# Constant matmuls ahead of the waits of TensorE in the first mixture attention

## The chip, the cores and the metric

The kernel runs on one core of one Trainium2 chip. The metric is the time of one execution in microseconds, median of several runs; less is better. TensorE computes the matmuls and transposes, ScalarE (ACT), VectorE (DVE) and GpSimd (POOL) work on the rows between them, and SyncE (SP) issues the transfers.

## What is computed

Eight sequences of 256 tokens with 256 features go through four layers: a gated fusion with a memory of 64 rows, a "mixture" block, a gated cross attention with a feed-forward part, and a second mixture block. The change touches the start of the first mixture block. Its first part is

```
x = rms_norm(hidden_states, ln_in_w)
mixed = where(vm, x @ v_qkv, x @ l_qkv)          # two experts, chosen by token
q, k, v = split(mixed)                            # 16 heads of 16
q, k = apply_rotary(q, k)
ctx = sdpa(q, k, v, causal=True)
hidden_states = residual + where(vm, ctx @ v_dense, ctx @ l_dense)
ci = rms_norm(hidden_states, ln_post_cross_w)     # then the cross attention on the memory
...
```

followed by a cross attention with 64 memory rows and a feed-forward part with two experts. All of it is in f32.

## The kernel before

Everything is kept with the features on the 128 partitions, so a sequence (an "element" e, 0 to 7 in the first mixture block, 8 to 15 in the second) is a tile of 128 x 2 x 256. The four layers run one after another in the main, but within a mixture block the stages of several elements are interleaved: norm (`n0_*`), projections (`q`, `k`, `v`), attention (`first_scores`, `turn_max`, `second_scores`, `values`), cross attention (`memory`, `dense`, `crs_*`, `cross_*`) and feed-forward (`up`, `down`).

The order is written out: each stage has a time in a table (`norm_stages`, `project_stages`, `attend_stages`, `cross_stages`, lines 210 to 597), each element a start, and `whole_order` (line 960) sorts all of them into one list. Every engine walks this list and issues the stages that are its own, in that order (`walk`, line 989). Between engines there are only semaphores: a stage waits (`wait_ge`) for counts of the stages whose results it reads or whose buffers it takes over.

On TensorE the order from the first norm of the first mixture block to its first cross attention is: n0_sum(0), n0_spread(0), q(0), k(0), v(0), n0_sum(1), n0_spread(1), first_scores(0,0), q(1), first_scores(0,1), k(1), first_scores(0,2), v(1), first_scores(0,3), n0_sum(2), n0_spread(2), turn_max(0), second_scores(0,0), second_scores(0,1), values(0,0), second_scores(0,2), values(0,1), second_scores(0,3), first_scores(1,0), values(0,2), values(0,3), first_scores(1,1), q(2), memory(0).

The names and lines that matter below:

- `n0_sum` (line 1450, matmuls at line 1442): sums of squares with the constant matrix `mean_w`, after POOL's addition (line 1241). DVE takes the mean (2233), POOL the power -1/2 (1250), `n0_spread` (1463, transposes at 1447) spreads it over partitions, DVE multiplies (2243) and splits by expert (2247, 2249).
- `q` (1467) and `k` (1482) go through `to_experts` (1421; matmuls at 1433 and, for the first expert, 1426), `v` (1491) through matmuls at 1495. In `q` of element 0, line 1470 reads eight values of the tile `early` into registers of TensorE's sequencer (`pe.value_load`), one for each sequence.
- `first_scores` (1507; 1527 and the causal mask at 1532) are made to find a maximum (DVE 2293), which `turn_max` (1536; transposes at 1545) brings to the other axis, and DVE (2300) subtracts inside the queries. `second_scores` (1548; 1560) are then exponentiated (ACT 2051), masked (POOL `select`, 1283), and multiplied with the values (`values`, 1565; 1577).
- `memory` (1584) is the first use of `crs_bank`, a bank of PSUM, in the mixture block. The loads of x use it before. `att_bank` holds sums, spreads, turned maxima and the attention's results.

Of the kernel before, what the change touches and what calls it, by code (L numbers as in the profile page):

```python
# [29 lines left out]
P = 128  # L30
# [139 lines left out]
def load_stages():  # L170

    at = []

    def put(time, stage, *which):
        at.append((time, stage, *which))

    put(-8637.7284, "x_out")
    put(4848.2942, "x_turn")
    return at


def fuse_stages():

    at = []

    def put(time, stage, *which):
        at.append((time, stage, *which))

    put(-9564.6366, "f_add")
    put(-9564.2232, "f_rstd")  # L190
    put(-780.2099, "f_shift")
    put(-779.9075, "f_sums")
    put(-772.2775, "f_gated")
    put(-771.5608, "f_mean")
    put(-771.0806, "f_y")
    put(-416.5783, "f_exp")
    put(-416.2034, "f_turn_out")
    put(-415.8700, "f_context_out")
    put(-413.5954, "f_tanh")
    put(-412.9521, "f_square")  # L200
    put(1545.6724, "f_scores")
    put(1546.6753, "f_turn")
    put(1547.0006, "f_context")
    put(1547.3799, "f_gate")
    put(1554.5187, "f_sum")
    put(1554.9323, "f_spread")
    return at
# [634 lines left out]
def keys_stages():  # L842

    at = []

    def put(time, stage, *which):
        at.append((time, stage, *which))

    put(-804.7289, "a_keys_out", 0)
    put(-804.4289, "a_keys_out", 1)  # L850
    put(1088.9990, "a_keys", 0)
    put(1089.0990, "a_keys", 1)
    return at
# [48 lines left out]
def final_stages():  # L902

    at = []

    def put(time, stage, *which):
        at.append((time, stage, *which))

    put(-9564.6367, "out_sent")
    put(-24.1953, "out")  # L910
    put(1485.6441, "turn_out")
    return at


def once_stages():

    at = []

    def put(time, stage, *which):
        at.append((time, stage, *which))  # L920

    put(-9125.4755, "p_vec_out")
    put(-9009.7270, "f_mem_out", 0)
    put(2269.6313, "p_one_hot")
    put(2270.2195, "p_trig_out")
    put(2272.2799, "p_seen")
    put(2455.0669, "a_zero")
    put(2634.1904, "f_mem_out", 1)
    put(2641.9461, "f_mem_out", 2)
    put(2642.8294, "f_mem_out", 3)  # L930
    put(4467.6526, "p_vec")
    put(4508.4445, "f_mem", 0)
    put(4596.4685, "p_trig")
    put(4597.0345, "f_mem", 1)
    put(4604.8206, "f_mem", 2)
    put(4605.0045, "f_mem", 3)
    return at
# [22 lines left out]
def whole_order():  # L960

    order = [(time, stage, 0, *which) for time, stage, *which in once_stages()]

    def each(starts, stages, first=0):
        for e in range(B):
            order.extend((starts[e] + time, stage, first + e, *which) for time, stage, *which in stages)

    def by_parity(starts, stages_of, layer):
        for e in range(B):
            order.extend((starts[layer][e] + time, stage, layer * B + e, *which) for time, stage, *which in stages_of(layer, e % 2))  # L970

    each(LOAD_STARTS, load_stages())
    each(FUSE_STARTS, fuse_stages())
    for layer in range(2):
        by_parity(NORM_STARTS, norm_stages, layer)
        by_parity(PROJECT_STARTS, project_stages, layer)
        by_parity(ATTEND_STARTS, attend_stages, layer)
        by_parity(CROSS_STARTS, cross_stages, layer)
        by_parity(FEED_STARTS, feed_stages, layer)
        order.extend((LATE_STARTS[layer][e // 2] + time, stage, layer * B + e, *which) for e in range(1, B, 2)  # L980
                     for time, stage, *which in late_stages(layer))
    each(FINAL_STARTS, final_stages(), B)
    each(GATED_STARTS, gated_stages())
    order.extend((KEYS_STARTS[e // 2] + time, stage, e, *which) for e in range(0, B, 2) for time, stage, *which in keys_stages())
    each(GATED_FF_STARTS, gated_ff_stages())
    return [(stage, e, *which) for _time, stage, e, *which in sorted(order)]
# [8 lines left out]
def program(nc, x_d, ctx_d, pos_d, type_d, media_d, fuse_w, mot_w, ca_w, const_d, out_d):  # L995
    ctx = ExitStack()
    with ctx:
        def sb(name, shape, dt=F32):
            return ctx.enter_context(nc.sbuf_tensor(name, shape, dt))
# [12 lines left out]
        mean_w = sb("mean_w", [P, P])  # L1012
# [155 lines left out]


        order = whole_order()  # L1170
        count = {n: [Count(section[n][e], order, n, e) for e in ENGINES] for n in SECTIONS}
        X_PE, X_ACT, X_DVE, _ = count["x"]
        F_PE, F_ACT, F_DVE, F_POOL = count["f"]
# [5 lines left out]
        OUT_PE, OUT_ACT, _, _ = count["out"]  # L1179
# [42 lines left out]
        with nc.Block() as block:  # L1222
# [151 lines left out]
            def _(pe):  # L1374
# [65 lines left out]
                def sum_squares(sq, out):  # L1440
                    for t in range(TT):
                        last = pe.matmul(out[:, t:t + 1], sq[:, 0, t * P:(t + 1) * P], mean_w[:, 0:1], start=True, stop=True)
                    return last
# [4 lines left out]
                    return last  # L1448

                def n0_sum(e):  # L1450
                    pe.wait_ge(*N0_POOL.did(e, "add"))
                    if e > 0:
                        pe.wait_ge(*N0_DVE.did(e - 1, "y"))
                    if e == 0:
                        pe.wait_ge(*F_ACT.did(0, "m3"))
                        pe.wait_ge(*X_ACT.did(B - 1, "x"))
                    elif e == B:
                        pe.wait_ge(*A_DVE.did(B - 1, "scaled"))
                    elif e % B > 2:
                        pe.wait_ge(*ATT_DVE.did(e - 3, "ctx1"))  # L1460
                    sum_squares(n0_sq, att_bank).then_inc(*N0_PE.does(e, "sumsq"))

                def n0_spread(e):
                    pe.wait_ge(*N0_POOL.did(e, "rstd"))
                    spread(n0_rs, att_bank).then_inc(*N0_PE.does(e, "spread"))

                def q(e):
                    if e == 0:
                        pe.wait_ge(*X_DVE.did(0, "early"))
                        has_early.extend(pe.value_load(early[0:1, b:b + 1]) for b in range(B))  # L1470
                    if e % B == 0:
                        pe.wait_ge(mot_in, 16 * MOT_DMAS * (e // B + 1))
                    if e % B > 3:
                        pe.wait_ge(*free_1(e - 4))
                    elif e % B > 0:
                        pe.wait_ge(*QKV_ACT.did(e - 1, "v1"))
                    if e == B or e == B + 1:
                        pe.wait_ge(*B_ACT.did(e - 2, "gelu2"))
                    pe.wait_ge(*N0_DVE.did(e, "yl"))
                    to_experts(e, ff_bank[1], qkv, 0, n0_yl, n0_yv, N0_DVE.did(e, "yv")).then_inc(*QKV_PE.does(e, "q"))  # L1480

# [52 lines left out]
                    last.then_inc(*ATT_PE.does(e, f"s1{w}"))  # L1534

                def turn_max(e):
                    pe.wait_ge(*ATT_DVE.did(e, "max3"))
                    if e % B + 2 < B:
                        pe.wait_ge(*N0_DVE.did(e + 2, "y"))
                    if e > 0:  # L1540
                        pe.wait_ge(*ATT_DVE.did(e - 1, "ctx1"))
                    for t in range(KT):
                        for i in range(TT):
                            at = t * S + i * P
                            last = pe.transpose(att_bank[:, at:at + P], neg_max[:, 2 * t + i, :], ident)
                    last.then_inc(*ATT_PE.does(e, "nm"))

                def second_scores(e, w):

                    t, par = w // 2, w % 2  # L1550
                    pe.wait_ge(*ATT_DVE.did(e, f"qa{par}"))
                    if w == 0:
                        if e > 0:
                            pe.wait_ge(*CRS_DVE.did(e - 1, "cmax1"))
                    else:
                        pe.wait_ge(*ATT_ACT.did(e, f"exp{w - 1}"))
                    for i in range(TT):
                        for j in range(4):
                            r = slice(32 * j, 32 * j + 32)
                            last = pe.matmul(row_banks[:, j, S * i:S + P * i], k_one[e % 2][par][r, t, i * P:(i + 1) * P],  # L1560
                                             q_one[e % 2][par][r, t, i * P:S], start=(i == 0), stop=(i == 1),
                                             skip_group_check=True)
                    last.then_inc(*ATT_PE.does(e, f"s2{w}"))
# [1042 lines left out]
```

## Time and profile before

| | us |
|---|---|
| median of 3 runs | 1384.76 |
| lowest, highest | 1384.41, 1391.71 |
| the profiled execution | 1382.84 |
| its span, first to last instruction | 1380.9 |
| TensorE busy in the span | 1306.9 (95%) |
| VectorE, ScalarE, GpSimd busy | 764.5, 473.6, 452.1 |
| mean granted clock of TensorE | 0.98 |

All times inside the execution are microseconds from its span's start. TensorE's busy time counts a matmul until its modelled end, so consecutive matmuls overlap; the chain of work gives the time that a group of them takes on the path. The granted clock is a share of 2.4 GHz: 1.00 is 2.4 GHz, 0.50 is 1.2 GHz, and a value between the two is a stretch with some of both. "Idle before" is the time that an engine stood still ahead of an instruction, with the engine that released it.

### The profile page before, as it was taken

Reading aid. Unit: us, or ns where it says so; the run is one execution under the profiler, and the core shown is the slowest. Engines: PE = TensorE matmul, PEld = TensorE weight load, DVE = VectorE, ACT = ScalarE, POOL = GpSimd, SP = SyncE. Lnnn points to the kernel's source line nnn. Section 1 sums busy time; section 2 is a strip of 40 time slices with the busy share of each in tenths; the row PEclk is TensorE's granted clock in tenths of the full one; section 3 lists DMA queues with packets and bytes.
Section 4 is the critical chain, followed back from the end, with each engine's and each line's share of the span. In section 5 each row is a group of like instructions: output and inputs, shape, how many; then the busy total and the mean of one; then the engine's idle time right before and its main releaser. Section 6 shows DMA issues by size and latency. Waiting matters only on the chain.

```text
span 1380.9 us, 25903 instructions
## 1 busy us (share of the span) xinstructions
PE 1306.9 (95%) x10931; PEld 1047.3 (76%) x10931; DVE 764.5 (55%) x1361; ACT 473.6 (34%) x785; POOL 452.1 (33%) x559
## 2 busy tenths in 40 slices
PE   7978899999999998999999999998899999999988
PEld 5755677787887776888888888876678777787767
DVE  4455576666666656354354444446667566666543
ACT  3323333423324222244445543433332333323321
POOL 1143444444344342311111111324434344334332
PEclk9978999999999999999999999999999999999999
DMA  9010000000001001110000000011000000000000
GB/s 324 8 61 1 2 2 2 1 2 2 2 2 47 2 5 48 50 60 1 0 1 1 1 0 1 1 42 42 1 2 1 9 9 2 1 17 2 1 16 17
DMA packets 19901, 27.29 MB, mean 20 GB/s; under 512 B 3432, under 2 KB 15552, under 8 KB 19520
## 3 DMA queue, kind: packets, MB, share of 16 engines
q1 hardware_dynamic: 19008, 24.20, 5.2%
q8 instruction: 99, 1.62, 0.5%
q10 hardware_dynamic: 768, 1.26, 0.3%
q14 instruction: 26, 0.21, 0.1%
HBM read 23.35 MB, written 2.10 MB: 18 GB/s over the span
## 4 chain that ended last, share of the span: by engine, by line
PE 84%; DVE 6%; ACT 5%; POOL 3%; issue 2%; ACTq 0%; DVEq 0%; POOLq 0%
PE bank L1433 6%; PE bank L1723 6%; PE bank L1688 5%; PE bank L1693 5%; PE bank L1577 5%; PE bank L1933 4%; PE bank L1940 4%; PE bank L1897 4%; PE row_banks L1527 4%; PE row_banks L1837 3%; PE row_banks L1560 3%; PE bank L1495 3%; PE bank L1712 3%; PE bank L1426 3%; PE row_banks L1532 2%; ACT room L2051 2%
## 5 line engine op out<-in xcount | busy, mean ns | idle before, releaser
L1283 POOL TENSOR_SCALAR_AFFINE_SELECT room<-room 128x1024 f32<-128x1024 f32 x64 | 70.7, 1107 | 185.3 <-ACT room L2051 185.3
L2293 DVE TENSOR_REDUCE room<-row_banks 128x4 f32<-128x512 f32 (+1 forms) x128 | 116.4, 952 | 23.1 <-PE row_banks L1532 22.8
L2051 ACT ACTIVATE room<-row_banks 128x1536 f32<-128x1536 f32 x64 | 92.9, 1451 | 90.0 <-PE row_banks L1560 90.0
L1723 PE MATMUL bank<-room,down_w 128*128 128x256 f32 x384 | 95.9, 391 | 0.5 <-DVE room L2393 0.5
L2307 DVE RECIPROCAL room<-bank 128x256 f32<-128x256 f32 x32 | 56.1, 1754 | 59.3 <-PE bank L1577 59.3
L2083 ACT ACTIVATE room<-bank 128x256 f32<-128x256 f32 x96 | 36.4, 383 | 148.6 <-PE bank L1693 137.6
L1245 POOL TENSOR_TENSOR room<-room 128x256 f32<-128x256 f32 x32 | 24.5, 767 | 173.0 <-ACT room L2063 173.0
L1723 PEld LDWEIGHTS bank<-room,down_w 128*128 128x128 f32 x384 | 70.4, 192 | 14.0 <-issue 4.9
L1357 POOL TENSOR_TENSOR room<-room 128x512 f32<-128x512 f32 x32 | 33.7, 1070 | 133.1 <-DVE room L2495 132.9
L1560 PE MATMUL row_banks<-room 32*128 32x256 f32 (+1 forms) x1024 | 62.1, 357 | 9.7 <-ACT room L2051 4.6
L1560 PEld LDWEIGHTS row_banks<-room 32*128 32x128 f32 x1024 | 48.9, 190 | 27.6 <-issue 15.6
L2376 DVE SCALAR_TENSOR_TENSOR room<-room,bank 128x256 f32<-128x256 f32 x96 | 39.9, 415 | 50.4 <-ACT room L2083 50.4
L1433 PE MATMUL bank<-room,qkv 128*128 128x256 f32 x256 | 64.0, 394 | 2.7 <-DVE room L2249 2.5
L2063 ACT ACTIVATE room<-x_all 128x512 f32<-128x512 f32 x32 | 20.2, 631 | 135.3 <-DVE x_all L2362 96.2
L1527 PE MATMUL row_banks<-room 32*128 32x128 f32 (+1 forms) x1024 | 62.9, 362 | 2.0 <-ACT room L2051 1.7
L1837 PE MATMUL row_banks<-room,wq 128*128 128x256 f32 x256 | 61.0, 382 | 0.0
L1940 PE MATMUL bank<-room,down_w 128*128 128x256 f32 x256 | 60.4, 380 | 0.0
L1933 PE MATMUL bank<-room,up_w 128*128 128x256 f32 x256 | 58.8, 382 | 1.0 <-ACT room L2169 1.0
L1897 PE MATMUL bank<-room,wo 128*128 128x256 f32 x256 | 59.6, 381 | 0.0
L1577 PE MATMUL bank<-room 128*32 128x256 f32 (+1 forms) x1024 | 55.9, 337 | 0.8
L1433 PEld LDWEIGHTS bank<-room,qkv 128*128 128x128 f32 x256 | 48.0, 196 | 10.5 <-issue 3.5
L1933 PEld LDWEIGHTS bank<-room,up_w 128*128 128x128 f32 x256 | 47.4, 190 | 9.3 <-ACT room L2169 2.5
(243 smaller groups left out, 3022.4 us busy)
## 6 DMA issues: line engine op xcount, KB each, us to landing
out_x<-wq SPq DMA_DIRECT2D x8, 256.0 KB, 2.4
qkv<-in_L_xattn_v_qkv SPq DMA_DIRECT2D x2, 768.0 KB, 5.6
qkv<-in_L_xattn_l_qkv SPq DMA_DIRECT2D x2, 768.0 KB, 8.6
gate_w<-in_L_xattn_v_gate SPq DMA_DIRECT2D x2, 640.0 KB, 8.0
gate_w<-in_L_xattn_l_gate SPq DMA_DIRECT2D x2, 640.0 KB, 7.4
up_w<-in_L_xattn_v_up SPq DMA_DIRECT2D x2, 640.0 KB, 6.1
up_w<-in_L_xattn_l_up SPq DMA_DIRECT2D x2, 640.0 KB, 6.4
down_w<-in_L_xattn_v_down SPq DMA_DIRECT2D x2, 640.0 KB, 6.0
```

What stands on the lines that cost most here:

```text
L1283: pool.affine_select(out=diagonal, in_=diagonal, compare_op=ALU.is_ge, fill=0.0, base=0, pattern=[[0, 8], [1, P]], channel_multiplier=-1)\
L1433: pe.matmul(out[:, t * S:(t + 1) * S], w[:, 1, k, at + t * P:at + (t + 1) * P], y_l[:, k, :], start=(t == k == 0), stop=False, skip_group_ ...
L1527: pe.matmul(row_banks[:, j, P * i:P + S * i], q_one[e % 2][par][r, t, i * P:(i + 1) * P], k_one[e % 2][par][r, t, 0:P * (i + 1)], start=(i ...
L1560: last = pe.matmul(row_banks[:, j, S * i:S + P * i], k_one[e % 2][par][r, t, i * P:(i + 1) * P], q_one[e % 2][par][r, t, i * P:S], start=( ...
L1577: last = pe.matmul(att_bank[32 * j:32 * j + 32, at + i * P:at + S], half if of_sums else v_pad[e % 2][:, i, 8 * t + 2 * j + par, :], probs ...
L1723: return pe.matmul(ff_bank[0][:, t * S:(t + 1) * S], down_w[:, f, t * P:(t + 1) * P], hid[:, i, :], start=(i == t == 0), stop=(i == UPS - ...
L1837: last = pe.matmul(row_banks[:, u, j * S:(j + 1) * S], wq[:, k, at:at + P], a_y[:, k, :], start=(k == 0), stop=(k == KT - 1))
L1897: last = pe.matmul(crs_bank[:, t * S:(t + 1) * S], wo[:, k, t * P:(t + 1) * P], a_context[:, k, :], start=(k == t == 0), stop=(k == GT - 1 ...
L1933: last = pe.matmul(ff_bank[(u + 1) % 2][:, j * S:(j + 1) * S], w1[:, k, at:at + P], b_y[:, k, :], start=(k == 0), stop=(k == KT - 1))
L1940: last = pe.matmul(crs_bank[:, t * S:(t + 1) * S], w2[:, k, t * P:(t + 1) * P], b_hid[:, k, :], start=(k == t == 0), stop=(k == GT - 1), s ...
L2051: act.activation(probs[w % 2], row_banks[:, :, 0:3 * P], ACT.Exp).then_inc(*ATT_ACT.does(e, f"exp{w}"))
L2293: last = dve.tensor_reduce(dst, row_banks[:, :, P * i:P + S * i], X, ALU.max, negate=True)
```

## The change

A helper `hold(n, ...)` issues n matmuls whose two operands are both `mean_w`, 128x128, into the first 128 columns of `crs_bank`. Nothing reads the result; `memory(0)` and later stages start new sums there. It issues them only for stages that stand between n0_sum(0) and memory(0) in the order, both excluded. The calls stand ahead of the stage's own waits, except in `q`, where the call stands behind the value loads and all waits but the last one.

```
+        lone = {key: n for n, key in enumerate(order)}
...
                 def n0_sum(e):
+                    hold(4, "n0_sum", e)
                     pe.wait_ge(*N0_POOL.did(e, "add"))
...
+                def hold(n, *key):
+                    if lone["n0_sum", 0] < lone[key] < lone["memory", 0]:
+                        for _ in range(n):
+                            pe.matmul(crs_bank[:, 0:P], mean_w[:], mean_w[:], start=True, stop=True)
+
                 def n0_spread(e):
+                    hold(3, "n0_spread", e)
                     pe.wait_ge(*N0_POOL.did(e, "rstd"))
...
                     if e == B or e == B + 1:
                         pe.wait_ge(*B_ACT.did(e - 2, "gelu2"))
+                    hold(6 if e == 0 else 3, "q", e)
                     pe.wait_ge(*N0_DVE.did(e, "yl"))
...
                 def turn_max(e):
+                    hold(4, "turn_max", e)
                     pe.wait_ge(*ATT_DVE.did(e, "max3"))
...
                 def second_scores(e, w):
+                    hold(4, "second_scores", e, w)
 
                     t, par = w // 2, w % 2
                     pe.wait_ge(*ATT_DVE.did(e, f"qa{par}"))
```

## Rows read from the trace of the kernel before

**Rows 1.** The page: granted clock in 40 slices, and the chain by engine.

```profile
PEclk9978999999999999999999999999999999999999
PE 84%; DVE 6%; ACT 5%; POOL 3%; issue 2%; ACTq 0%; DVEq 0%; POOLq 0%
```

**Rows 2.** Busy time by stretch: columns in the first line.

```profile
core 0: us, PE busy (x) PEld busy (x) DVE busy (x) ACT busy (x) POOL busy (x), PEclk, DMA share, GB/s
84.90:87.30 2.40, 0.00 (x0) 0.00 (x0) 2.23 (x4) 0.00 (x0) 0.00 (x0) 0.50 1.00 413
91.00:91.50 0.50, 0.50 (x6) 0.50 (x4) 0.00 (x0) 0.00 (x0) 0.00 (x0) 0.76 0.00 0
98.00:101.00 3.00, 0.88 (x6) 0.71 (x6) 1.36 (x2) 3.00 (x9) 1.73 (x3) 1.00 0.00 0
101.00:101.50 0.50, 0.18 (x6) 0.05 (x4) 0.31 (x1) 0.38 (x1) 0.00 (x0) 0.98 0.00 0
104.50:105.00 0.50, 0.50 (x3) 0.41 (x2) 0.50 (x2) 0.00 (x0) 0.00 (x0) 0.60 0.14 33
115.10:118.30 3.20, 2.02 (x25) 1.30 (x24) 0.95 (x3) 3.08 (x8) 1.43 (x2) 1.00 0.00 0
118.50:119.00 0.50, 0.38 (x2) 0.04 (x1) 0.50 (x1) 0.50 (x1) 0.00 (x0) 0.55 0.00 0
128.50:129.00 0.50, 0.50 (x16) 0.18 (x8) 0.00 (x0) 0.10 (x1) 0.34 (x1) 0.71 0.00 0
132.20:135.60 3.40, 1.75 (x35) 1.23 (x30) 1.72 (x2) 1.45 (x1) 1.80 (x2) 1.00 0.02 5
163.00:169.50 6.50, 4.86 (x50) 2.99 (x50) 0.88 (x2) 2.90 (x2) 2.18 (x2) 0.50 0.00 0
995.00:1003.00 8.00, 5.95 (x33) 4.01 (x34) 6.52 (x13) 0.74 (x2) 3.80 (x4) 0.57 0.00 0
```

**Rows 3.** The value loads of line 1470, and the instructions in time beside them.

```profile
L1470 PEldq TENSOR_LOAD <-early x8: 301/306/496, 84.1 to 86.9; - x8
84.15 0.69 PE L1447 MATMUL bank<-const,room 128*128 128x128 f32 x2 [1.03 <-POOL room L1250]
86.51 0.69 DVE L2249 TENSOR_TENSOR room<-room 128x512 f32<-128x512 f32 x1
87.38 0.76 PE L1433 MATMUL bank<-room,qkv 128*128 128x256 f32 x1 [2.54 <-DVE room L2249]
```

**Rows 4.** TensorE's instructions in time: start, duration, count, [idle before, releaser].

```profile
99.08 0.61 PE L1442 MATMUL bank<-mean_w,room 128*128 128x1 f32 x4 [1.74 <-POOL room L1241]
101.48 1.67 PE L1527 MATMUL row_banks<-room 32*128 32x128 f32 x16 [0.32 <-ACT room L2041]
...
103.90 2.39 PE L1433 MATMUL bank<-room,qkv 128*128 128x256 f32 x8
...
116.71 0.61 PE L1442 MATMUL bank<-mean_w,room 128*128 128x1 f32 x4 [0.20 <-POOL room L1241]
...
120.17 1.09 PE L1545 MATMUL bank<-const,room 128*128 128x128 f32 x4 [1.29 <-DVE room L2243]
122.10 1.67 PE L1560 MATMUL row_banks<-room 32*128 32x256 f32 x16 [0.84 <-DVE room L2300]
125.42 1.67 PE L1560 MATMUL row_banks<-room 32*128 32x256 f32 x16 [1.66 <-ACT room L2051]
...
129.30 0.94 PE L1560 MATMUL row_banks<-room 32*128 32x256 f32 x16
...
131.90 0.94 PE L1560 MATMUL row_banks<-room 32*128 32x256 f32 x16 [0.22 <-ACT room L2051]
```

**Rows 5.** Chain of work (start, us, what), and one select of POOL.

```profile
266.54 1.98 PE bank L1712 x16
127.09 2.28 PE bank L1577 x32
179.89 1.30 PE bank L1577 x32
125.35 1.10 POOL L1283 TENSOR_SCALAR_AFFINE_SELECT room<-room 128x1024 f32<-128x1024 f32 x1 [7.06 <-ACT room L2051]
```

More of the change, by code:

```diff
@@ L1170, in program @@
         order = whole_order()
+        lone = {key: n for n, key in enumerate(order)}
         count = {n: [Count(section[n][e], order, n, e) for e in ENGINES] for n in SECTIONS}
@@ L1450, in n0_sum @@
                 def n0_sum(e):
+                    hold(4, "n0_sum", e)
                     pe.wait_ge(*N0_POOL.did(e, "add"))
@@ L1461, in n0_sum, with hold @@
                     sum_squares(n0_sq, att_bank).then_inc(*N0_PE.does(e, "sumsq"))
+                def hold(n, *key):
+                    if lone["n0_sum", 0] < lone[key] < lone["memory", 0]:
+                        for _ in range(n):
+                            pe.matmul(crs_bank[:, 0:P], mean_w[:], mean_w[:], start=True, stop=True)
                 def n0_spread(e):
+                    hold(3, "n0_spread", e)
                     pe.wait_ge(*N0_POOL.did(e, "rstd"))
@@ L1478, in q @@
                         pe.wait_ge(*B_ACT.did(e - 2, "gelu2"))
+                    hold(6 if e == 0 else 3, "q", e)
                     pe.wait_ge(*N0_DVE.did(e, "yl"))
@@ L1536, in turn_max @@
                 def turn_max(e):
+                    hold(4, "turn_max", e)
                     pe.wait_ge(*ATT_DVE.did(e, "max3"))
@@ L1548, in second_scores @@
                 def second_scores(e, w):
+                    hold(4, "second_scores", e, w)
                     t, par = w // 2, w % 2
```

## The prediction

> **What bounds the kernel now.** The page comes first. The chain of work that ended last is 84% TensorE, and the granted clock is at full speed in nearly every slice; the only slices below nine tenths lie early, between about 70 and 175 us [rows 1]. So time is lost to the clock only in a few places, and time on TensorE's path is mostly paid one for one. Next I cut the early part into short stretches to see where the clock changes level [rows 2]. It is low already over 84.9 to 87.3, rises inside 91.0 to 91.5, is low again from 101.5 to inside 104.5 to 105.0, falls inside 118.5 to 119.0 and rises inside 128.5 to 129.0, and is low over 163.0 to 169.5. Low is 1.2 GHz (0.50), high 2.4 GHz (1.00). Taking each change inside its row by the row's mean clock, the first low ends at about 91.3, the second is 101.5 to 104.9 and the third 118.6 to 128.8. Ahead of the second one TensorE was busy for 0.88 of 3.0 us, and ahead of the third for 2.02 of 3.2 us [rows 2]. These lows are what the products could remove. Last I read the instructions of TensorE in order with the idle time ahead of each [rows 3, 4], since a product is free only if it lies in such an idle time.
>
> **Which products run where.** The order of stages puts these between the first sum and the first cross attention: spread(0) 3, q(0) 6, sum(1) 4, spread(1) 3, q(1) 3, sum(2) 4, spread(2) 3, turn_max(0) 4, second_scores(0, 0 to 3) 4 each, q(2) 3: 49 in all.
>
> **Price of one.** A product is a 128x128 f32 weight load and a 128-column f32 matmul. The nearest row is the run of sixteen such matmuls of L1712 at the high clock: 1.98 us, 0.124 us each [rows 5]. At the low clock I take twice that, 0.248, since the same second-score group costs 1.67 us low and 0.94 high [rows 4]. So three cost 0.37, four 0.50, six 0.74 at the high clock. All 49 would be 6.1 us high, 12.2 low; nothing hidden is the upper bound, all hidden the lower.
>
> **Products that gaps hide.** Each spread waits 1.03 us for the power on POOL (one of three alike stands in rows 3): three products fit even at the low clock (0.74). Sum(1) waits 1.74 us, four fit. Turn_max(0) waits 1.29, second_scores(0,0) 0.84, second_scores(0,1) 1.66 [rows 4]: 0.50 each fits at the high clock; at the low one (0.99) the middle of these would stick out by 0.15. Cost: nothing. Without that cover each would cost its 0.37 or 0.50.
>
> **Products that nothing hides.** q(0) looks as if it had a gap of 2.54 us, but the sequencer is not free in it: has_early reads eight values, 0.30 us each, the first at 84.1 and the last at 86.9 [rows 3], so they end at about 87.2. The six products stand behind them in the order. The splitting on DVE that q(0) waits for also ends at 87.20 (86.51+0.69) [rows 3]. So the gap is covered by the loads, and the six start when q(0) would have. They run at the low clock, 1.49 us. The first low stretch has begun before the first product, and the 2.4 us without any TensorE work [rows 2] stay, so I let the clock rise at 91.3 as before. Then 1.49 us of low work is pushed out and an equal amount of q(0) moves beyond the rise, at half its price: the delay is 0.74. The bounds are 0 (the rise comes earlier by that much) and 1.49 (it moves along). From v(0) to the first scores of element 0 the chain carries this 0.74. These scores would start at 102.2 in place of 101.48, still in the second low. That stretch then does 0.74 us less of slow work, which refunds 0.37.
> q(1) and q(2) follow the group before them with no idle time (one of the two stands in rows 4): 0.37 each. Sum(2) waits only 0.20 [rows 4]: 0.50 less 0.20 is 0.30, and what waits behind it is spread(2), and on DVE the mean, which stands ahead of the last maximum of element 0 and so of turn_max. Second_scores(0,2) has no idle time ahead of it: 0.50. Its exp on ACT waits with it. Second_scores(0,3) has 0.22 [rows 4]: 0.28. Sum of what is paid: 0.74 - 0.37 + 0.37 + 0.30 + 0.50 + 0.28 + 0.37 = 2.19 us.
>
> **What the clock gives back.** First low: nothing, as said. Second low: I expect it to stay. In the 4 us between v(0) and the first scores (97.3 to 101.5) TensorE gets seven products, 0.87 us, beside 0.88 us of its own small matmuls in 98 to 101 [rows 2], and most of it remains without work. If it did go, the scores would take what such a group takes at the high clock, 0.94 rather than 1.67 [rows 4], and the rest of the stretch, 1.8 us, would halve: in all 1.7 us less, minus the 0.37 already counted. Third low: I expect it to go. Ahead of it TensorE had 2.02 of 3.2 us; the four products of sum(2) and three of spread(2) close 0.87 of the rest, and the following idle times (1.29, 0.84, 1.66) get 0.50 each. Its price, on the path: turn_max 1.09 against some 0.55 (half), 0.55; second_scores(0,0) 1.67 against 0.94, 0.73; second_scores(0,1) ends 0.73 earlier too, but values(0,0) waits for the select on POOL, which is what comes late next (exp ends at about 125.3, select takes 1.10 from 125.35 on [rows 5], so values could start near 126.5 in place of 127.09): 0.58. Values(0,0), 2.28 against 1.30 for the same 32 matmuls at the high clock [rows 5]: 0.98. Together 2.84 us.
> **Net: 2.19 - 2.84 = -0.65 us.** The path behind is PE's again, so it carries to the end.
>
> A rule of the skill speaks about the matmuls that lie in these gaps already. Rows show the clock low over transposes that are busy for part of a gap [rows 4]. The Trainium skill, "TensorE: Matmul & The Clock Gate", Part 4, says that transposes don't count as TensorE activity the way matmuls do. By that the ordinary products here do more for the clock than the transposes beside them, which agrees with the third low going; no row of before separates the two.
>
> **The time.** The profiled execution took 1382.84 us (span 1380.9 and 1.9 around it), 1.9 below the median of the runs shown, 1384.76. By the profile's own time the change gives 1382.2; on the median 1384.1. I forecast the median, 1384.1.
>
> **Rivals.**
> (a) *The products cost, and the clock is no better* (slower). One mechanism, at the third low: it stays, or returns a few us later. For it: each idle time there (1.29, 0.84, 1.66) gets only 0.50 of products, so TensorE still stands still between the groups. Against it: at 132.2 to 135.6 the clock stayed high over idle times of 0.22 and 1.65 between the same groups (1.75 of 3.4 us busy) [rows 2]. Then the 2.19 are paid, and 0.15 for second_scores(0,0): +2.3, 1387.1. It decides as soon as the clock returns less than 2.2 us.
> (b) *More lows go.* The second (1.7 - 0.4 = 1.3 us), and the one at 163.0 to 169.5, in which TensorE is busy for 4.86 us at half speed [rows 2], 2.4 us at most. It lies behind the last product, and only a shift in time can move it: ahead of it DVE holds TensorE up for 3 us, which argues that it stays. Both: -0.65 - 1.3 - 2.4 = -4.4, 1380.4.
> (c) *The lows are not tied to the program.* The profiled execution alone shows where the clock changed; it was 1.9 us faster than the median, and other runs may have their lows elsewhere. The Trainium skill, the same page, "What's actually happening", says the point of change is not set by the kernel's start and varies. A shift of the later part by half a us can then also make or unmake a low such as the one within 995.0 to 1003.0 [rows 2], where TensorE was busy for 5.95 us at a mean clock of 0.57: each is worth 1.7 us or so either way. That puts the time at 1381 to 1389 with no trend.
> (d) *The change does not do what it says at q(0)*: its six products lie behind the value loads and not in the gap. That is in my sum already; if the loads ended earlier, or the low ended earlier because of them, the time would be 0.4 to 0.7 lower, 1383.5.
>
> **How the numbers follow.** Forecast (with d) 0.50, (a) 0.22, (b) 0.18, (c) 0.10. About 0.5% (6.9 us) is what a measurement of this kernel can tell from no change. Neither -4.4 nor +2.3 reaches it; only several lows together with (c) do, in either direction: faster 0.05, slower 0.04, same 0.91. The range goes from (b) to (a) with one further low of 1.7: 1380.4 to 1388.8. Its ends leave 2 in 10 out, mostly for disturbances like the third run of before, 1391.71.
>
> **What would show it.** In the profile of after: matmuls of 128x128 with mean_w in the bank of the cross attention, 49 of them; q(0)'s first true matmul at about 88.6 and not 87.4 (right: the loads cover the gap); the clock rising near 91.3 and low again near 101.5 to 104.9; high from 104.9 past 128.8, with turn_max at 0.55 and second scores at 0.94 (wrong: 1.09 and 1.67); second_scores(0,2) starting 0.5 after values(0,0) ends; q(2) about 0.7 us earlier than 139.95. Wrong in kind would be idle times that grow by what the products take, a low clock at new places behind 170, or a product price far from 0.12.

## The result and the profile after

| | before | after |
|---|---|---|
| median, 12 runs each | 1384.45 us | 1388.64 us |
| lowest, highest | 1383.31, 1392.04 | 1384.81, 1389.82 |
| the profiled execution (its span) | 1382.84 (1380.9) | 1386.58 (1384.6) |
| TensorE matmuls in the trace | 10931 | 11029 |

The ratio is 1.0025, with a 95% interval of 1.0014 to 1.0035: the change costs some 3.5 us, clear of noise and below the 0.5% that I had called telling. The two medians differ by 4.2 us, and the two profiled executions, one of each kernel, by 3.7 us. These two can be compared piece by piece. The twelve times of after fall in two groups, five from 1384.8 to 1386.6 with a mean granted clock of 0.984 to 0.986 and seven from 1388.6 to 1389.8 with 0.982 or 0.983. The profiled one is the slowest of the first group, so its trace doesn't show what the second group adds.

The page of after, its granted clock in 40 slices and the first line of the chain:

```profile
PEclk9989899999999999999999999999999999999999
PE 84%; DVE 6%; ACT 4%; POOL 3%; issue 2%; DMA 0%; SPq 0%; ACTq 0%; DVEq 0%; POOLq 0%
```

They answer [rows 1]: the same bound, and no slice below eight tenths where before had one at seven. The stretches of after answer [rows 2] (columns as there):

```profile
79.30:92.60 13.30, 10.40 (x39) 8.66 (x39) 5.19 (x12) 0.00 (x0) 3.01 (x5) 0.50 0.42 158
93.00:136.90 43.90, 39.30 (x399) 32.38 (x398) 21.84 (x34) 15.98 (x26) 17.64 (x16) 1.00 0.00 1
134.20:137.00 2.80, 1.22 (x20) 0.88 (x20) 0.25 (x1) 1.44 (x1) 1.09 (x1) 1.00 0.00 0
137.00:140.50 3.50, 3.50 (x43) 1.98 (x44) 1.83 (x2) 0.00 (x0) 0.00 (x0) 0.53 0.03 5
167.80:174.60 6.80, 6.33 (x66) 4.20 (x66) 0.88 (x2) 1.78 (x2) 2.19 (x2) 0.51 0.00 0
```

The clock is high without a break from 93.0 to 136.9: both lows that the products surround, near 101 and 118, are gone. The first is as long as before. A new one runs from 137.0 to 140.5, and the one that was at 163 is at 168. So up to the cross attention the clock did better than forecast, one low more gone against a short new one, and the time did worse.

Where it went is in the line of the products and in the chain (start, us, what). First the products' own row, all from the matmul call inside `hold` at L1468 (durations min/median/max in ns, first and last start):

```profile
L1468 PE MATMUL bank<-mean_w x98: 273/275/561, 83.2 to 143.5; 128*128 128x128 f32 x98
```

```profile
85.28 2.19 issue
87.47 2.90 PE bank L1468 x12
90.37 3.01 PE bank L1434 x8
...
105.10 0.67 PE bank L1468 x6
...
118.03 0.89 PE bank L1468 x8
...
122.12 0.63 PE bank L1555 x4
122.75 0.89 PE bank L1468 x8
123.64 0.93 PE row_banks L1571 x16
...
128.78 1.09 PE bank L1468 x8
129.86 0.86 PE row_banks L1571 x16
130.73 1.44 PE bank L1588 x32
132.17 1.09 PE bank L1468 x8
...
137.26 4.41 PE bank L1588 x64
...
143.08 0.67 PE bank L1468 x6
```

The 49 products are 98 matmuls in the trace. The six of q(0) are "x12" and take 2.90 us; four are "x8" and take 0.89, 0.22 each. An f32 matmul is two records here, each with its own weight load (98 weight loads too). A transpose in f32 is one: the two that line 1447 issues are x2 in [rows 3]. I had read "L1712 x16" of [rows 5] as sixteen products at 0.124; by the loops of that line (2 tiles, 2 weight matrices, 2 halves of the contraction) they are eight at 0.248.

How far the execution of after lies behind that of before, at starts of the same work. All but the first row are read from the two chains; the cross attention is taken from the second group of matmuls of memory(0), L1594 in before and L1605 in after. The first row is ahead of the first product; its lines, of before and of after:

```profile
82.10 1.01 PE L1442 MATMUL bank<-mean_w,room 128*128 128x1 f32 x4
82.35 1.01 PE L1443 MATMUL bank<-mean_w,room 128*128 128x1 f32 x4
```

| start of | before | after | behind by |
|---|---|---|---|
| n0_sum(0) | 82.10 | 82.35 | 0.25 |
| q(0) | 87.38 | 90.37 | 2.99 |
| first scores of 0 | 101.48 | 103.62 | 2.14 |
| next first scores | 107.12 | 108.64 | 1.52 |
| turn_max(0) | 120.17 | 122.12 | 1.95 |
| second_scores(0,0) | 122.10 | 123.64 | 1.54 |
| values(0,0) | 127.09 | 127.27 | 0.18 |
| second_scores(0,3) | 131.90 | 133.25 | 1.35 |
| values(0,2) | 135.97 | 137.26 | 1.29 |
| q(2) | 140.11 | 143.75 | 3.64 |
| the cross attention | 142.90 | 146.54 | 3.64 |
| the end | 1380.9 | 1384.6 | 3.7 |

Two things made it: the products that nothing covered, and 1.67 us for the new low (values(0,2) and (0,3): 4.41 for 2.74). What the second and the third low gave back was not enough for both: the lag falls by 0.62 from the first scores of 0 to the next, with the 0.67 of q(1)'s products paid inside, and by 1.77 from turn_max(0) to values(0,0). 0.25 us of the lag has nothing to do with the products, since it is there before the first of them. By the cross attention the loss is complete.

### The profile page after: what moved, and what is told of

The parts are those of the page before. It is cut to its first block, busy times and chain, and to the rows that moved or that the text cites. A ratio compares the mean times of both kernels' runs of the same rounds, so it can differ in the third digit from the quotient of the medians.

```text
span 1384.6 us, 26096 instructions
## 1 busy us (share of the span) xinstructions
PE 1317.5 (95%) x11029; PEld 1058.5 (76%) x11029; DVE 764.6 (55%) x1361; ACT 474.1 (34%) x785; POOL 452.9 (33%) x559
## 4 chain that ended last, share of the span: by engine, by line
PE 84%; DVE 6%; ACT 4%; POOL 3%; issue 2%; DMA 0%; SPq 0%; ACTq 0%; DVEq 0%; POOLq 0%
PE bank L1434 6%; PE bank L1734 6%; PE bank L1699 5%; PE bank L1588 5%; PE bank L1704 5%; PE bank L1944 4%; PE bank L1951 4%; PE bank L1908 4%; PE row_banks L1536 4%; PE row_banks L1848 3%; PE row_banks L1571 3%; PE bank L1504 3%; PE bank L1723 3%; PE bank L1427 3%; PE row_banks L1541 2%; PE row_banks L1882 2%
## 5 line engine op out<-in xcount | busy, mean ns | idle before, releaser
L1588 PE MATMUL bank<-room,const 128*32 128x256 f32 (+1 forms) x1024 | 54.7, 332 | 0.0
```

The lines of the kernel that those rows point to most:

```text
L1588: last = pe.matmul(att_bank[32 * j:32 * j + 32, at + i * P:at + S], half if of_sums else v_pad[e % 2][:, i, 8 * t + 2 * j + par, :], probs ...
```

## The experiments

Each kernel has its own runs of before beside it on the same chip, and only the ratio compares kernels: the medians of before were 1383.66 beside e1 to e4, 1383.72 beside e5 to e8, 1384.61 beside e9 to e11 and 1383.43 beside e12. Two theories were put against each other. P: the loss is the price of the products that no gap covers, at twice what I had taken. C: it is a matter of where the clock falls, and only by chance related to what is paid.

| kernel | median, us | ratio to before | 95% interval | n0_sum(0) | cross attention | from the one to the other | from there to the end |
|---|---|---|---|---|---|---|---|
| before | 1384.45 |  |  | 82.10 | 142.90 | 60.80 | 1238.0 |
| the change | 1388.64 | 1.0025 | 1.0014, 1.0035 | 82.35 | 146.54 | 64.19 | 1238.1 |
| e1 covered products only | 1382.79 | 0.9996 | 0.9987, 1.0005 | 82.50 | 142.82 | 60.32 | 1237.8 |
| e2 uncovered only | 1392.74 | 1.0069 | 1.0055, 1.0083 | 82.37 | 149.04 | 66.67 | 1237.9 |
| e3 q(0)'s six ahead of the loads | 1383.27 | 0.9997 | 0.9983, 1.0010 | 80.91 | 141.52 | 60.61 | 1238.1 |
| e4 16 at k(1) | 1387.24 | 1.0028 | 1.0018, 1.0039 | 82.64 | 147.35 | 64.71 | 1238.0 |
| e5 covered and early six | 1379.72 | 0.9976 | 0.9962, 0.9991 | 81.02 | 137.20 | 56.18 | 1237.9 |
| e6 the same, and first_scores(1,0) | 1377.98 | 0.9963 | 0.9950, 0.9977 | 82.21 | 138.38 | 56.17 | 1237.8 |
| e7 the same, and the fusion | 1377.92 | 0.9965 | 0.9953, 0.9977 | 81.97 | 138.42 | 56.45 | 1241.4 |
| e8 all in bf16 | 1386.47 | 1.0024 | 1.0015, 1.0033 | 81.93 | 144.62 | 62.69 | 1237.9 |
| e9 without q(0)'s six | 1386.52 | 1.0021 | 1.0011, 1.0030 | 81.69 | 145.14 | 63.45 | 1238.6 |
| e10 the early six only | 1385.73 | 1.0012 | 0.9996, 1.0027 | 82.94 | 146.01 | 63.07 | 1242.3 |
| e11 e6 again | 1382.10 | 0.9982 | 0.9967, 0.9998 | 82.02 | 138.26 | 56.24 | 1238.0 |
| e12 the change and first_scores(1,0) | 1389.24 | 1.0038 | 1.0026, 1.0050 | 82.51 | 144.46 | 61.95 | 1242.5 |

The last four columns are from each kernel's one profiled execution, which is any one of its runs. n0_sum(0) stands ahead of the first product (in e7 only, some stand ahead of it), and its start still lies between 80.91 and 82.94 from one execution to another, though the kernels do the same up to there. So what a kernel does to the stretch with the products is read from the last column but one, not from where the cross attention starts. Behind the cross attention eleven of the fourteen executions take the same 1237.8 to 1238.6 us, and those of e7, e10 and e12 take 1241.4 to 1242.5.

**The price.** All products of the change out, sixteen ahead of k(1), between two groups at the high clock:

```
                 def k(e):
+                    if e == 1:
+                        hold(16, "k", e)
```

> None of the change's products; 16 of them stand ahead of k(1), between two full groups of matmuls at the high clock. This measures the price by itself. By the corrected count (two passes per f32 product, 0.22 us): 3.6 us above before. By the prediction's 0.124: 2.0 us above before.

The chain of e4 around them:

```profile
108.87 0.54 PE row_banks L1540 x4
109.41 3.57 PE bank L1467 x32
112.98 1.73 PE bank L1434 x8
```

3.57 us for sixteen, 0.223 each, and the time went up by 0.28%, 3.9 us (interval 0.18 to 0.39%, 2.5 to 5.4 us). From n0_sum(0) to the cross attention the profiled execution took 3.91 us longer than that of before. The price is twice 0.112, and it is paid in full: nothing behind gives it back.

**Covered and uncovered apart.** e1 keeps the 25 products of which a gap covers all or nearly all:

```
-                    hold(4, "n0_sum", e)
+                    hold(4 if e == 1 else 0, "n0_sum", e)
...
-                    hold(6 if e == 0 else 3, "q", e)
...
-                    hold(4, "second_scores", e, w)
+                    hold(4 if w < 2 else 0, "second_scores", e, w)
```

> Only the 25 products of the changed kernel that a gap covers stay (spread(0), sum(1), spread(1), spread(2), turn_max(0), second_scores(0,0) and (0,1)); the 24 that stand where TensorE has other work are left out. Theory P (the loss is the price of the uncovered products, about 0.22 us each at the high clock and 0.48 at the low): at most 0.3 us is paid, and if the lows near 101 and 118 us still go, the time is 1 to 4 us below the kernel before, ratio 0.997 to 0.999. Theory C (the loss is where the clock falls afterwards, whatever is paid): within 1 us of before or above it.

e2 is the other half: the calls of e1 out, and in their place only `hold(4 if e == 2 else 0, "n0_sum", e)`, the call in `q`, and `hold(4 if w > 1 else 0, "second_scores", e, w)`.

> Only the 24 products that no gap covers (q(0) 6, q(1) 3, sum(2) 4, second_scores(0,2) and (0,3) 4 each, q(2) 3). Theory P: all of the price and little of the clock, so slower than the full change: 5 to 7 us above before, ratio 1.004 to 1.005. Theory C: the same lows as before or others by chance, 0 to 4 us above before, not above the full change.

Three stretches of e1, then two of e2:

```profile
102.60:105.60 3.00, 3.00 (x22) 1.80 (x17) 2.44 (x5) 0.00 (x0) 0.00 (x0) 0.50 0.00 0
107.00:132.00 25.00, 22.37 (x265) 17.54 (x263) 13.44 (x20) 10.20 (x15) 9.70 (x9) 1.00 0.01 1
133.20:136.40 3.20, 3.20 (x35) 1.55 (x32) 1.14 (x2) 0.00 (x0) 0.64 (x1) 0.50 0.02 5
```

```profile
102.20:108.80 6.60, 6.23 (x33) 4.61 (x34) 4.08 (x6) 0.82 (x2) 0.11 (x1) 0.50 0.01 2
126.00:132.70 6.70, 5.06 (x64) 3.30 (x56) 1.48 (x3) 2.90 (x2) 1.95 (x2) 0.50 0.00 0
```

In e1 the second low stays and the third is gone, exchanged for a shorter one at 133 where before had none. It is as fast as before within noise. P had said 1 to 4 us less, and C within 1 us of before: C's number came true. From the first sum to the cross attention it took 0.48 us less than before: the new low takes most of what the old one gave. In e2 both lows stay, and it is 0.7% slower, 9 us, more than P's 5 to 7 and far from C's 0 to 4. Its profiled execution, 1388.88, is the fastest of its five runs. There the stretch with the products took 5.87 us longer, which is P's number; the other four runs (1392.4 to 1393.2) took some 4 us more, and no trace shows where. So the uncovered half is the loss; 5.9 of e2's 9 us are seen to be the products'.

**The six of q(0).** e3 moves them ahead of the value loads, e9 leaves them out, e10 keeps them early and nothing else.

```
                 def q(e):
                     if e == 0:
+                        hold(6, "q", e)
+                    if e == 0:
                         pe.wait_ge(*X_DVE.did(0, "early"))
                         has_early.extend(...)
...
-                    hold(6 if e == 0 else 3, "q", e)
+                    if e:
+                        hold(3, "q", e)
```

> The full change with the six products of q(0) ahead of the eight value loads. Theory P: they then run in the 2.5 us in which the sequencer reads values, 2.9 us of low-clock work of which some 2.5 is covered; q(0) starts near 88 and not 90.4, and the time is 1.5 to 2.5 us below the full change. Theory C: no change beyond 1 us unless the first low ends earlier.

> The full change without the six products of q(0), 43 left. If those six cost only their own time, 2.9 us of low-clock work of which part is given back after the rise, this lies 1.5 to 2.5 us below the full change, near 1386.5 (ratio 1.001 to 1.002). If the place ahead of the value loads helped e3_early6 also by ending the first low sooner, e3_early6 stays 2 to 3 us below this one. If both are equal, the gain of e3_early6 was the removal alone.

> The kernel before with only the six products ahead of the value loads. If they end the first low sooner by themselves, q(0) takes 1 to 1.7 us less and the time is 1 to 2 us below before, ratio 0.9985 to 0.9995. If they need the three of spread(0) beside them, the low lasts as before and the 0.4 us that stick out are lost, ratio 1.000.

e3's value loads, its products and q(0) in time, the clock around them, and e3's own new low:

```profile
L1480 PEldq TENSOR_LOAD <-early x8: 296/302/492, 83.1 to 85.8; - x8
```

```profile
83.20 0.64 PE L1448 MATMUL bank<-const,room 128*128 128x128 f32 x2
83.63 2.77 PE L1468 MATMUL bank<-mean_w 128*128 128x128 f32 x12
86.35 2.10 PE L1434 MATMUL bank<-room,qkv 128*128 128x256 f32 x8
```

```profile
83.80:86.30 2.50, 2.50 (x13) 2.30 (x11) 2.26 (x4) 0.00 (x0) 0.00 (x0) 0.50 1.03 421
86.50:87.00 0.50, 0.50 (x3) 0.45 (x4) 0.00 (x0) 0.00 (x0) 0.00 (x0) 0.86 1.04 442
131.00:134.30 3.30, 3.30 (x32) 1.66 (x36) 0.87 (x2) 0.00 (x0) 0.88 (x1) 0.50 0.02 5
```

Once the products stand ahead of them, TensorE works through the twelve matmuls while its sequencer reads the eight values: the loads start at 83.1, the products run from 83.63, and q(0) follows without a gap. In before q(0) starts 5.28 us behind the start of n0_sum(0), in the change 8.02 and in e3 5.49. In before it runs at the low clock for 3.75 us (chain), in e3 it takes 2.06, since the clock rises near 86.6; all five traces with these six and the three of spread(0) have 2.06 to 2.34. That is worth more than the removal, as the runs show: e9, with the six left out, gains 0.04% on the change, e3 0.28%, 3.9 us. For e9 1.5 to 2.5 us had been expected, for e3 the same; from n0_sum(0) to the cross attention they took 0.74 and 3.58 us less than the change. The six are not enough by themselves: in e10's profiled execution the first low lasts to 89.5 or a little more, the second is longer than in before, and one comes at 137.5 to 141.0 with no product near it. Its time is that of before or a little over it. That execution, 1390.26, is one of the slower ones of e10, whose median is 1385.73, so these lows are not those of most of its runs:

```profile
80.00:89.50 9.50, 7.96 (x30) 6.42 (x30) 5.19 (x12) 0.00 (x0) 2.90 (x5) 0.50 0.47 179
100.00:107.00 7.00, 6.47 (x30) 4.31 (x31) 4.08 (x6) 1.12 (x2) 0.41 (x1) 0.51 0.01 2
120.50:130.50 10.00, 6.85 (x68) 4.64 (x68) 3.20 (x6) 2.90 (x2) 1.96 (x2) 0.50 0.00 0
```

**Shorter products.** e8 takes `ident_bf` for both operands of all 49.

> The full change with all 49 products in bf16 (the identity of bf16 on both sides): one pass each rather than two, so about 0.06 us at the high clock. Theory P: the uncovered ones cost a quarter to a half of what they did, so 2 to 5 us below the full change, 1384 to 1386; if the clock falls as in the full change, the lows near 101 and 118 us stay away. Theory C: the time depends on the lows alone and stays near 1388; with shorter products the lows may come back.

```profile
L1468 PE MATMUL bank<-ident_bf x49: 216/219/314, 82.8 to 141.6; 128*128 128x128 bf16 x49
101.20:104.40 3.20, 2.99 (x24) 2.12 (x25) 2.52 (x5) 0.11 (x1) 0.00 (x0) 0.50 0.00 0
121.60:128.30 6.70, 5.57 (x60) 3.93 (x64) 1.90 (x3) 2.90 (x2) 1.22 (x2) 0.50 0.00 0
135.30:138.50 3.20, 3.20 (x35) 1.72 (x36) 1.83 (x2) 0.00 (x0) 0.12 (x1) 0.50 0.02 5
```

One record a product, and a quarter to a half of the price (the four of sum(2): 0.22 us in its chain). But the low at 101 is back and most of that at 118, a new one follows at 135, and the ratio is that of the full change within noise. P had the price right and the clock wrong; what the products cost less, the clock takes back for the most part. In the profiled executions 1.5 us are left of it from n0_sum(0) to the cross attention (62.69 us for 64.19).

**Which products remove which low.** The second low, near 101, is gone in the seven traces with six f32 products at q(0), in either place, and the seven of sum(1) and spread(1) (the change, e3, e5, e6, e7, e11, e12). It is there in e1 and e9, which have the seven alone, in e2 and e10, which have the six alone, and in e8, whose products are short. So it takes both; why the six help over 10 us later is not shown. A new low of some 3 us between 131 and 141 comes in the change, e1, e3, e8, e9 and e10.

**Only what is covered.** e5 is e1 with the six of e3. e6 adds `hold(6, "first_scores", e, w)` for w = 0, e = 1, in the 1.66 us ahead of the new low. e7 adds to e6 six products between the fusion's last sums and spreads, and one wait ahead of them for the last read of the bank.

> The 25 covered products plus the six of q(0) ahead of the value loads; the other 18 left out. Theory P: what was paid for the uncovered ones is gone (of the early six about 0.4 us stays), and the first low can end earlier: 1 to 3 us below before, ratio 0.998 to 0.999, and below both parts alone. Theory C: as the two parts alone, within 1 us of before.

> As the run before it, and six more products ahead of first_scores(1,0), where TensorE waits 1.66 us for the exp and where a new low began in the full change (137 us) and in e1_hidden (133 us). Theory P with the new low as its missing term: that low doesn't come, worth about 1.7 us: 1380 or a little less, ratio 0.997 to 0.998. If the low only moves on to the next idle time, no gain over the run before it.

> As the run before it, and six more products in the idle times of the fusion's last sums and spreads (75 to 82 us), of 0.45 to 0.6 us each. If the first low is due to these idle times, it doesn't come at all, and q(0) runs at the high clock: another 1 to 2 us less. If the 2 us of waiting ahead of q(0) bring it anyway, nothing is gained, and the products that stick out cost up to 0.5 us.

Stretches of e5:

```profile
80.50:86.50 6.00, 6.00 (x27) 5.39 (x27) 3.50 (x8) 0.00 (x0) 1.17 (x2) 0.50 0.55 208
95.00:100.00 5.00, 3.58 (x37) 2.63 (x36) 2.69 (x5) 3.72 (x9) 2.07 (x3) 1.00 0.00 0
100.00:115.00 15.00, 13.88 (x117) 10.93 (x115) 9.90 (x17) 4.16 (x10) 6.35 (x6) 1.00 0.01 1
115.00:135.00 20.00, 16.86 (x266) 12.66 (x267) 10.41 (x13) 6.72 (x6) 4.44 (x5) 1.00 0.01 2
```

The first low is short and there is none up to 135: the cross attention starts 5.7 us sooner than before, and this execution ends 5.8 sooner (1375.1 for 1380.9). 1.1 us of this was there at n0_sum(0) (81.02 for 82.10), ahead of all products, so they are worth 4.6. e5's other runs spread from 1376.86 to 1388.43, so its ratio shows less, 0.24%, 3.3 us, a little more than the 1 to 3 expected. e6 and e7 come out at 0.9963 and 0.9965, as fast as each other: the products in the fusion bring nothing. e11 is e6 once more:

> The kernel of e6_hid_early_fs once more, in other runs, to see whether its gain holds: ratio 0.995 to 0.9977 as there. If its lows were placed by chance, the ratio goes back toward 0.998.

It gave 0.9982, and the two intervals share only 0.9967 to 0.9977. That e6 is faster than before holds in both; its gain is 0.2 to 0.4%, not surely the 0.37% of the first time. e5 lies between the two, so the times leave open whether the products at first_scores(1,0) help. In the traces they bring nothing: from n0_sum(0) to the cross attention e5 took 56.18 us, e6 56.17 and e11 56.24, and e5 has no low between 87 and 158 without them.

**The new low.** e12 is the full change with those six at first_scores(1,0).

> The full change with six more products ahead of first_scores(1,0), in the 1.66 us behind the last second scores, ahead of the new low at 137 us. If that low comes from this idle time, it goes, values(0,2) and (0,3) take 2.74 and not 4.41 us, and the time is about 1.7 us below the full change, near 1387 (ratio 1.001 to 1.002). If it only moves to a later place, the time is that of the full change, ratio 1.0025.

```profile
137.00:140.50 3.50, 3.50 (x81) 2.35 (x74) 2.56 (x3) 0.00 (x0) 0.00 (x0) 1.00 0.00 0
508.00:511.50 3.50, 3.50 (x11) 2.85 (x11) 0.00 (x0) 0.00 (x0) 0.00 (x0) 0.54 0.00 0
532.00:539.00 7.00, 6.22 (x24) 4.63 (x28) 2.07 (x3) 0.59 (x1) 1.48 (x3) 0.51 0.00 0
904.00:911.00 7.00, 5.03 (x30) 3.68 (x31) 1.64 (x5) 5.09 (x8) 2.08 (x3) 0.51 0.00 0
```

Its place was right: the low at 137 is gone, and the cross attention starts at 144.46, 2.1 us sooner than in the change, as the expectation had it. And yet e12 is not faster: 1.0038, where 1.001 to 1.002 was expected. Lows that neither before nor after has begin at 508 and at 532, with no product near them, and the one at 904 lasts 7 us (in before 3 to 4). From the cross attention to the end e12 took 4.4 us longer than the change. e7 and e10 have such lows too, near 525 and 533 and at 897 and 905, and took 3.3 and 4.2 us longer there. Here C has its part, and not by where the later work falls: e7 reaches the cross attention at the same time as e6 and e11 to 0.2 us, and these two have no such lows.

## Why the prediction was wrong

I forecast 1384.1, 0.65 us better; measured was 1388.64, some 3.5 worse. It is inside my range, near the end, on the wrong side of no change, and within the 0.5% to which I gave 0.91.

- *The term that failed is the price of one product*, 0.124 us in my sum. It measured 0.223 in e4 and in after, 0.48 at the low clock. The count of a row is of records, and an f32 matmul has two. [Rows 4] could have told me: `second_scores` issues eight matmuls and its row says x16, and the values' row says x32 for sixteen. With 0.223 in my own sum, what is paid is 1.34 - 0.67 (half refunded in the second low) + 0.67 + 0.69 + 0.89 + 0.67 + 0.67 = 4.3 us for my 2.19, and the net 4.3 - 2.8 = +1.4. So the price alone turns the sign. With the 1.67 of the new low it is 3.1; from n0_sum(0) to the cross attention the change took 3.39 us more than before.
- *What nothing hides* was named right in every place, and e2 shows that it is the loss. q(0)'s gap is covered by the value loads, as I said: q(0) began at 90.4. I had 88.6 (my own price gives 87.38 + 1.49 = 88.9, a slip), off by the price again. The six took 2.90 us, and the lag of 2.99 shrank to 2.14 at the first scores, rather than my 1.49 and 0.74.
- *What gaps hide* held mostly, with a thinner margin. Products of four are 0.89 us, so those of second_scores(0,0) stand out of their 0.84 a little. The three of spread(0) did not fit: at the low clock they take 1.49 for a wait of 1.03, and spread(0) ended 0.43 behind the last of them. In e1, which has them and not the six, q(0) started 0.16 later for it.
- *First low*: not shortened, right (it lasts at least 13.3 us in after, to inside 92.5 to 93.0 where before had 91.0 to 91.5). *Third low*: gone, right; values(0,0) did come out limited by the select on POOL, and the lag fell from 1.95 to 0.18 us from turn_max to there, against 2.84 - 0.98 = 1.86 of my sum up to that point. *Second low*: I expected it to stay, and it went. That products twice as long filled its gap is not the whole reason: e1 and e9, with the same seven products there but without the six of q(0), kept it.
- *The new low* at 137 to 140.5 was missing from my sum, 1.67 us: the second term that failed. I had used the idle times there as evidence that the clock holds [rows 2]. It held in one execution and, 1.3 us later in time, didn't in the next. What sets it off is open: six traces have one there, and e10 without a product near it.
- Rival (a) had the sign right and a size (2.3 us) nearer than mine, in part for the wrong reason: the third low did go. But a low came back a few us later, as (a) has it. Rival (c), that lows move with no tie to the products, is what the lows behind 500 us in e7, e10 and e12 show, and the two groups of times agree with it. The Trainium skill, "TensorE: Matmul & The Clock Gate", "What's actually happening", says that the point at which the clock changes varies between runs of one kernel. The mean clocks of the twelve runs of the change, which range from 0.982 to 0.986, agree. The prediction's sentences on transposes were not put to a test by any run.
- Rival (d) asked for an earlier end of the loads or of the first low, and neither came in the change. What the place is worth was undervalued there at 0.4 to 0.7: ahead of the loads, the same six products turned a loss of 3.5 us into nothing (e3) and, with the uncovered ones out, into a gain of 3 to 4 (e5).

What stays open: why a low appears between 508 and 540 in some executions, why the six of q(0) bear on the low near 101, and what the slower group of the change's runs has more, as none of them was profiled. That the median of the change is 4.2 us over before's and not 1 us, as its faster group alone would be, hangs on this group.

## What to carry to other kernels

Before costing a matmul from a row, count the matmuls of its source lines and compare with the row's count; in f32 the rows here have two for one, and one for a transpose. Filling TensorE's gaps to hold its clock pays only where the gap is one of the array and not of its queue: put the filler ahead of what the sequencer does in the gap, and leave it out wherever TensorE goes straight on. A low that is removed may be followed by one a little later, so ask what the next idle time is. Compare times over many runs, and in profiles compare the length of the stretch that you changed, not the time at which it ends: one execution may start it 1 to 2 us sooner than another.

## What the runs showed of the hardware

Reading eight values into registers takes TensorE's sequencer 0.30 us each, some 3 us from the first start to the last end, and the array works on beside it if its matmuls were issued first (e3: loads start at 83.1 to 85.8, matmuls run from 83.63 to 86.4). An f32 product of 128x128 by 128 columns takes 0.22 us at 2.4 GHz (e4, 3.57 us for sixteen) and 0.48 at 1.2 GHz (2.90 us for the six of q(0)); in bf16 it takes some 0.06 (e8, 0.22 us for four). So f32 costs four times as much, though it has only two records. The executions of the change fall in two groups some 3 to 4 us apart, and the group with the higher mean granted clock is the faster one; within a group the clock doesn't order the times (1386.58 at 0.986, 1384.81 at 0.985).
